# Self-attention scores by one mixed matrix, two-byte self parts, and an earlier load of two biases

## The reference

```python
# x: [1, 2048, 256]; every part is x = x + part(layernorm(x))
input_norm = norm(h, axis=-1); scaled = h / (input_norm + 1e-9)
q = scaled @ Wq.T + bq;  v = scaled @ Wv.T + bv
scores = q @ (q @ A).T / sqrt(256)                 # one head, width 256
ctx = softmax(scores) @ v;  out = ctx * input_norm
# cross-attention: 4 heads of width 64, keys and values from ctx_1024
# feed-forward: idx = argmax(softmax(x @ Wg + bg));  y = gelu(x @ W1[idx] + b1[idx]) @ W2[idx] + b2[idx]
```

## Time and profile before

| | |
|---|---|
| median of 3 runs | 823.52 us (822.39 to 825.96) |
| profiled execution | 824.94 us, of which the span of instructions 823.0 us |
| mean granted TensorE clock | 0.977 of full speed |
| PE busy | 760.4 us (92%) |
| PEld busy | 686.0 us (83%) |
| DVE busy | 629.1 us (76%) |
| ACT busy | 457.3 us (56%) |
| POOL busy | 165.5 us (20%) |

### The profile page before, as it was taken

The page is one execution under the profiler, slowest core; times in us unless marked ns, Lnnn a source line. Parts: engine busy times, 40 slices in busy tenths (PEclk is TensorE's granted clock), DMA queues, the critical chain, the costliest instruction groups (busy, mean ns, idle before and its releaser), DMA issues. The chain is left out here.

```text
span 823.0 us, 19881 instructions
## 1 busy us (share of the span) xinstructions
PE 760.4 (92%) x6226; PEld 686.0 (83%) x6227; DVE 629.1 (76%) x1608; ACT 457.3 (56%) x930; POOL 165.5 (20%) x254
## 2 busy tenths in 40 slices
PE   3878889999999999999999999999997768999996
PEld 2768779899898898988988889899895657999996
DVE  4983746797898888888889888888886754777773
ACT  2554536666766667666666666666664612444342
POOL 3100121212303123031230312303212011222221
PEclk9999989999999999999999999999999959999999
DMA  6233233213233131231312314213189290111110
GB/s 218 72 106 108 64 131 121 102 33 109 61 112 106 38 111 62 97 106 38 123 61 85 106 38 131 76 62 106 39 288 368 88 335 27 37 41 39 39 33 15
DMA packets 51146, 80.94 MB, mean 98 GB/s; under 512 B 4894, under 2 KB 29216, under 8 KB 50976
## 3 DMA queue, kind: packets, MB, share of 16 engines
q1 hardware_dynamic: 49232, 75.63, 27.2%
q0 software_dynamic: 1872, 4.76, 1.6%
HBM read 45.60 MB, written 35.18 MB: 98 GB/s over the span
## 5 line engine op out<-in xcount | busy, mean ns | idle before, releaser
L1135 ACT ACTIVATE ps_cross<-flip 128x512 f16<-128x512 f32 (+1 forms) x256 | 124.8, 515 | 110.4 <-PE flip L847 89.3
L1360 DVE TENSOR_TENSOR ps_cross<-flip,ps_cross 128x512 f16<-128x512 f32 (+1 forms) x256 | 145.0, 584 | 29.4 <-ACT ps_cross L1135 28.5
L1321 ACT ACTIVATE exp_cross<-exp_cross,xneg 128x1024 f32<-128x1024 f32 (+1 forms) x128 | 122.7, 960 | 28.0 <-DVE xneg L1520 28.0
L847 PE MATMUL flip<-ident,exp_cross 128*128 128x128 f32 (+1 forms) x832 | 130.9, 280 | 6.7 <-DVE ps_cross L1360 3.6
L836 PE MATMUL scores<-keys_cross,qt 128*128 128x402 f32 x512 | 126.8, 369 | 4.9 <-DVE xneg L1520 3.1
L847 PEld LDWEIGHTS flip<-ident,exp_cross 128*128 128x128 f32 (+1 forms) x832 | 95.2, 142 | 14.2 <-DVE ps_cross L1360 5.1
L724 PE MATMUL scores<-keys_self,u_tile 128*128 128x512 f32 x384 | 102.2, 403 | 4.3 <-issue 2.4
L823 PE MATMUL flip<-vals_self,ps_self 128*128 128x256 f32 x768 | 104.1, 290 | 0.0
L858 PE MATMUL cross_out<-vals_cross,ps_cross 128*128 128x128 f16 (+1 forms) x832 | 100.6, 222 | 0.2 <-DVE ps_cross L1360 0.2
L823 PEld LDWEIGHTS flip<-vals_self,ps_self 128*128 128x128 f32 x768 | 97.2, 195 | 0.0
L860 PE MATMUL cross_out<-vals_cross,ps_cross 128*128 128x64 f16 (+1 forms) x832 | 94.0, 194 | 0.0
(11 more groups left out here) (199 smaller groups left out, 1210.4 us busy)
## 6 DMA issues: line engine op xcount, KB each, us to landing
rows_dram<-pads SPq DMA_DIRECT2D x17, 520.0 KB, 4.0
w_piece<-W SPq DMA_DIRECT2D x32, 256.0 KB, 2.9
w_dram<-w_high SPq DMA_DIRECT2D x32, 256.0 KB, 2.3
w_dram<-w_piece SPq DMA_DIRECT2D x32, 256.0 KB, 2.7
w1s<-w_dram SPq DMA_DIRECT2D x8, 1024.0 KB, 12.4
w2s<-w_dram SPq DMA_DIRECT2D x8, 1024.0 KB, 12.5
...
```

Source lines behind the costliest of these rows:

```text
L847: tr = pe.transpose(flip[0:rows, bank(use), n * P:(n + 1) * P], exp_cross[:, h % 2, m * P:m * P + rows], ident[:, :])
L1135: return act.activation(out, in_, ACT.Copy, **kw)
L1321: act.activation(exp_cross[:, h % 2, cols], exp_cross[:, h % 2, cols], ACT.Exp, bias=xneg[:, h % 2, 1:2], scale=-1.0, accum_out=xden[:, ha ...
L1360: return dve.tensor_tensor(out, full, hi, ALU.subtract)
```

## The change

The score q A q' is written as x (Wq' A Wq) x' with a bias: in the prologue TensorE transposes Wq, multiplies A's matrix with it (`mixed[:, 0]`) and that with Wq again (`mixed[:, 1]`, with the factor 1/16), each with high and low parts, and two small products give u's bias `mixed_bias`. The parts of the transposed rows themselves are the keys: `xt_pro` goes, ScalarE and VectorE write them to `keys_self`, and the key matmuls and their parts go. u is mixed x x plus its bias. The values of group 0 come between the two products, and the statistics of group 1 ahead of the scaling of group 0.

`vals_self` and `ps_self` hold two-byte parts. The values are scaled by a number from a bound on them (row sums of squares of Wv, a sum over partitions by a matmul, a square root on GpSimd, the largest bv), the probabilities by 16384; the norms are multiplied by the inverse. `ps_self` has four buffers. b1 and b2 are loaded right after the prologue, behind the first piece's load, in a space of their own.

```diff
@@ -145,10 +146,11 @@
-    vals_self = sb("vals_self", [P, T, 2, D], F32R, keep)
+    vals_self = sb("vals_self", [P, T, 2, D], F16, keep)
+    exp_self = sb("exp_self", [P, N], F32, keep)
+    ps_self = sb("ps_self", [P, 4, 2, 512], F16, keep)
...
...
@@ -498,6 +510,8 @@
+        sp.dma_start(b1_row[:, :], bass.AP(io["b1"].tensor, 0, [[0, P], [1, E * DF]])).then_inc(b_loaded, 16)
+        sp.dma_start(b2_row[:, :], bass.AP(io["b2"].tensor, 0, [[0, P], [1, E * D]])).then_inc(b_loaded, 16)
...
@@ -547,8 +561,6 @@
-        sp.dma_start(b1_row[:, :], bass.AP(io["b1"].tensor, 0, [[0, P], [1, E * DF]])).then_inc(b_loaded, 16)
-        sp.dma_start(b2_row[:, :], bass.AP(io["b2"].tensor, 0, [[0, P], [1, E * D]])).then_inc(b_loaded, 16)
...
@@ -614,6 +626,9 @@
         for g in range(4):
+            if g == 2:
+                pool.wait_ge(bound_step, 3)
+                pool.tensor_tensor(v_bound[:, 2:3], v_bound[:, 1:2], plus_half[:, 0:1], ALU.pow).then_inc(bound_rooted, 1)
...
@@ -741,35 +758,68 @@
         def flip_x_pro(g):
-                pe.wait_ge(rows_scaled, 4 * (g + 1))
+                    pe.wait_ge(rows_scaled, 4 * (g + 1))
+                    if g == 0:
+                        pe.wait_ge(rows_scaled, n + 1)
+        pe.wait_ge(self_w_loaded, 48)
+        for c in range(C):
+            for o in range(C):
+                tr = pe.transpose(scores[:, 0, o * D + c * P:o * D + (c + 1) * P], w_raw[:, 0, c, o * P:(o + 1) * P], ident[:, :])
+        tr.then_inc(wq_flipped, 1)
-        for g in range(GROUPS):
-            if g == 0:
-                pe.wait_ge(self_w_lo, 1)
-            pe.wait_ge(pro_xt_lo, C * (g + 1))
-            for o in range(C):
-                if g:
-                    pe.wait_ge(pro_q_lo, C * (g - 1) + o + 1)
-                three(scores[:, o, :], lambda a, c: w_self[:, 0, a, c, o * P:(o + 1) * P],
-                      lambda b, c: xt_pro[:, g % 2, b, c, :]).then_inc(pro_q_ready, 1)
+        pe.wait_ge(self_w_lo, 2)
+        for o in range(C):
+            mm = three(scores[:, 1, o * D:(o + 1) * D], lambda a, c: w_self[:, 2, a, c, o * P:(o + 1) * P],
+                       lambda b, c: w_self[:, 0, b, c, :])
+        mm.then_inc(mixed_ready, 1)
+        def self_v(g):
+            for n in range(4):
+                if g == 0:
+                    pe.wait_ge(self_w_lo, 3)
+                pe.wait_ge(pro_xt_lo, C * (g + 1))
+                if g and n % 2 == 0:
+                    pe.wait_ge(pro_v_biased, 4 * (g - 1) + n + 2)
+                three(scores[:, 2 + n // 2, (n % 2) * D:(n % 2 + 1) * D],
+                      lambda a, c: keys_self[:, a, c, (4 * g + n) * P:(4 * g + n + 1) * P],
+                      lambda b, c: w_self[:, 1, b, c, :]).then_inc(pro_v_ready, 1)
+        self_v(0)
+        pe.wait_ge(mixed_lo, 1)
+        for o in range(C):
+            mm = three(scores[:, 0, o * D:(o + 1) * D], lambda a, c: mixed[:, 0, a, c, o * P:(o + 1) * P],
+                       lambda b, c: w_self[:, 0, b, c, :])
+        mm.then_inc(mixed_ready, 1)
+        pe.wait_ge(bound_step, 2)
+        pe.matmul(cross_out[:, 0:1], ones[:, :], bound16[:, :], start=True, stop=True).then_inc(bound_summed, 1)
...
+        for o in range(C):
+            for c in range(C):
+                mm = pe.matmul(cross_out[:, 8 + o:9 + o], w_raw[:, 2, c, o * P:(o + 1) * P], bq_col[:, c:c + 1],
...
+        mm.then_inc(bias_mixed, 1)
+        flip_x_pro(1)
+        pe.wait_ge(mixed_bias_set, 1)
+        pe.wait_ge(bound_step, 3)
+        for o in range(C):
...
+            for c in range(C):
+                for part in range(2):
+                    mm = pe.matmul(cross_out[:, 16 + o:17 + o], w_self[:, 0, part, c, o * P:(o + 1) * P].bitcast(F32),
+                                   mixed_bias[:, 0, c:c + 1], start=(n == 0), stop=(n == 3))
...
+        mm.then_inc(bias_mixed, 1)
+        self_u(0)
+        for g in range(1, GROUPS):
+            self_v(g)
-            if g == 0:
-                pe.wait_ge(self_w_lo, 2)
-            for n in range(4):
-                if g and n % 2 == 0:
-                    pe.wait_ge(pro_v_biased, 4 * (g - 1) + n + 2)
-                three(scores[:, 2 + n // 2, (n % 2) * D:(n % 2 + 1) * D] , lambda a, c: xt_pro[:, g % 2, a, c, n * P:(n + 1) * P],
-                      lambda b, c: w_self[:, 1, b, c, :]).then_inc(pro_v_ready, 1)
...
@@ -820,7 +870,7 @@
-                    mm = pe.matmul(self_out[:, 0:D], ps_self[:, g % 3, a, n * P:(n + 1) * P], vals_self[:, m, b, :],
+                    mm = pe.matmul(self_out[:, 0:D], ps_self[:, g, a, n * P:(n + 1) * P], vals_self[:, m, b, :],
...
@@ -1135,8 +1185,10 @@
-        for n in range(3):
-            copy(w_self[:, n, 0, :, :], w_raw[:, n, :, :]).then_inc(self_w_hi, 1)
+        copy(w_self[:, 2, 0, :, :], w_raw[:, 2, :, :]).then_inc(self_w_hi, 1)
+        act.wait_ge(wq_flipped, 1)
+        copy(w_self[:, 0, 0, :, :], scores[:, 0, :].rearrange("p (c n) -> p c n", c=C)).then_inc(self_w_hi, 1)
+        copy(w_self[:, 1, 0, :, :], w_raw[:, 1, :, :]).then_inc(self_w_hi, 1)
...
@@ -1144,29 +1196,28 @@
-                act.activation(u_out[:, :, o, :], out[:, :].rearrange("p (t s) -> p t s", t=4), ACT.Copy,
-                               scale=1.0 / 16.0).then_inc(u_hi_ready, 1)
+                act.wait_ge(mixed_bias_set, 2)
+                act.activation(u_out[:, :, o, :], out[:, :].rearrange("p (t s) -> p t s", t=4), ACT.Identity,
+                               bias=mixed_bias[:, 1, o:o + 1]).then_inc(u_hi_ready, 1)
         def xt_hi_pro(g):
...
-                copy(xt_pro[:, g % 2, 0, c, :], flip[:, c, :]).then_inc(pro_xt_hi, 1)
+                copy(keys_self[:, 0, c, g * 512:(g + 1) * 512], flip[:, c, :]).then_inc(pro_xt_hi, 1)
-        act.wait_ge(biases_loaded, 64)
+        act.wait_ge(mixed_ready, 1)
+        copy(mixed[:, 0, 0, :, :], scores[:, 1, :].rearrange("p (c n) -> p c n", c=C)).then_inc(mixed_hi, 1)
+        act.wait_ge(mixed_ready, 2)
+        copy(mixed[:, 1, 0, :, :], scores[:, 0, :].rearrange("p (c n) -> p c n", c=C), scale=1.0 / 16.0).then_inc(mixed_hi, 1)
         for g in range(GROUPS):
-            for o in range(C):
-                act.wait_ge(pro_q_ready, C * g + o + 1)
-                act.activation(keys_self[:, 0, o, g * 512:(g + 1) * 512], scores[:, o, :], ACT.Identity,
-                               bias=bq_col[:, o:o + 1]).then_inc(pro_q_hi, 1)
-                copy(vals_self[:, 4 * g + n, 0, :], v_tmp[:, n % 2, :]).then_inc(pro_v_hi, 1)
+                act.wait_ge(self_scale_step, 2)
+                act.activation(vals_self[:, 4 * g + n, 0, :], v_tmp[:, n % 2, :], ACT.Copy,
+                               scale=self_scale[:, 0:1]).then_inc(pro_v_hi, 1)
...
@@ -1219,11 +1270,9 @@
         def self_hi(j, k, g):
-            if g == 3:
-                act.wait_ge(self_p_used, 4 * j + 1)
-            elif k >= 1:
-                act.wait_ge(self_p_used, 4 * j if g == 0 else 4 * j + g - 3)
-            copy(ps_self[:, g % 3, 0, :], flip[:, bank(("s", g)), :]).then_inc(self_p_hi, 1)
+            if k >= 1:
+                act.wait_ge(self_p_used, 4 * j + g - 3)
+            copy(ps_self[:, g, 0, :], flip[:, bank(("s", g)), :], scale=P_TOP).then_inc(self_p_hi, 1)
...
@@ -1390,39 +1439,64 @@
         def xt_lo_pro(g):
-                low(xt_pro[:, g % 2, 1, c, :], flip[:, c, :], xt_pro[:, g % 2, 0, c, :].bitcast(F32)).then_inc(pro_xt_lo, 1)
+                low(keys_self[:, 1, c, g * 512:(g + 1) * 512], flip[:, c, :],
+                    keys_self[:, 0, c, g * 512:(g + 1) * 512].bitcast(F32)).then_inc(pro_xt_lo, 1)
-                                         scalar=1.0 / 16.0, in1=u_out[:, :, o, :].bitcast(F32), op0=ALU.mult,
+                                         scalar=mixed_bias[:, 1, o:o + 1], in1=u_out[:, :, o, :].bitcast(F32), op0=ALU.add,
-        for n in range(3):
-            if n == 1:
-                scale_rows(0)
-            dve.wait_ge(self_w_hi, n + 1)
-            low(w_self[:, n, 1, :, :], w_raw[:, n, :, :], w_self[:, n, 0, :, :].bitcast(F32)).then_inc(self_w_lo, 1)
-            if n == 1:
-                xt_lo_pro(0)
-                statistics_pro(1)
+        statistics_pro(1)
+        scale_rows(0)
+        dve.wait_ge(self_w_hi, 1)
+        low(w_self[:, 2, 1, :, :], w_raw[:, 2, :, :], w_self[:, 2, 0, :, :].bitcast(F32)).then_inc(self_w_lo, 1)
+        dve.wait_ge(self_w_hi, 2)
+        low(w_self[:, 0, 1, :, :], scores[:, 0, :].rearrange("p (c n) -> p c n", c=C),
+            w_self[:, 0, 0, :, :].bitcast(F32)).then_inc(self_w_lo, 1)
+        xt_lo_pro(0)
+        dve.wait_ge(self_w_hi, 3)
+        low(w_self[:, 1, 1, :, :], w_raw[:, 1, :, :], w_self[:, 1, 0, :, :].bitcast(F32)).then_inc(self_w_lo, 1)
+        dve.wait_ge(mixed_hi, 1)
+        low(mixed[:, 0, 1, :, :], scores[:, 1, :].rearrange("p (c n) -> p c n", c=C),
+            mixed[:, 0, 0, :, :].bitcast(F32)).then_inc(mixed_lo, 1)
```

(98 more changed lines are left out.)

9 lines of the change are left out of this document (4 added, 5 removed).

## The result

The changed kernel took **826.85 us** (median of 20 runs) against 822.68 us (median of 20 runs of the kernel before): **1.0036 times** the time before, with a 95% interval of 1.0025 to 1.0047, or +3.0 us. The ratio leaves disturbed executions out, the medians don't. The forecast was 823.2 us and no change: the time lies inside the range, but the slowing was not forecast. The profiled execution took 824.5 us (span 822.3, granted clock 0.968), 0.4 us *less* than the one of before.

The account below looks back on a forecast made before the run. Steady tiles were taken as bound by TensorE's self_values ahead of x1, the prologue by VectorE's queue, then a DMA round. Front +4.9, self parts -5.2, biases 0: -0.3, forecast 823.2 us, no change; range 817.8 to 830.

Parts of the forecast that it names:

- biases in tile 0: Loading b1 and b2 early on SP's queue in tile 0: 6.7 us at 389 GB/s, u_tile(1) in time, cost 0.
- The burst holds tile 1: Rival: the early b1 and b2 loads make tile 1's scores wait, +6 us, 829.2 us; chance 0.04.
- Self parts: Steady tiles: two-byte self_values matmuls at 113 ns for 120 save 0.31 us a tile ahead of x1, -5.2 us together.
- two bytes no faster: Rival, 48 self_values matmuls a tile: still 118 ns or more apart, so -5.2 is lost, 828.4 us; chance 0.14.
- Front: Prologue up to tile 0's start: mixing chain and reordered statistics, less key work, make it +4.9 us later (+2.5 to +7.6).
- the walk: Prologue followed along VectorE's queue: group 0 ends at 40.2 (+5.2), group 1 +4.45, u's high part of group 3 +4.65.
- the clock's 1.25 us: Rival on the prologue: TensorE idles longer and gets 1.2 GHz, forecast as +2.9 us, 826.1 us; chance 0.12.
- The sum's base: Whole kernel: -0.3 on the profiled 824.94 us gives 824.6; that execution lies 1.4 over the median 823.52, so 823.2.

## Why the prediction was wrong, point by point

**The step that failed** is the one on the biases in tile 0: "Cost 0." It measured 0.0037 in the changed kernel (1.0036 for 0.9999) and 0.0059 in the kernel with 2-byte parts: 3 to 5 us, all of the change's loss. I followed SP's own queue to u_tile(1), and that was nearly right: that load took 10.5 us to land and was there at 117.0 (forecast 112), ahead of the scores at 120.6. What I never listed was who else had DMAs in flight. GpSimd's four stores are another queue, and the chain from them (GpSimd's low part, the piece's stores, the next piece, ScalarE's copy, q's parts) was already tight: in the trace of before, ScalarE's copy of piece 1 ended 25.7 us after the first scores and q's high part began at 25.6. There the wait for x1 of tile 0 held the piece's load, and the stores were 1.6 us ahead of it. "The burst holds tile 1" stood as a rival at 0.04, with the wrong path and 6 us where it was 3 to 5. Its chance was too small because I asked only whether the bytes fit, and by full bandwidth at that: 389 GB/s, where the 2 MB took 11.1 us to land.

**Self parts**: forecast -5.2, measured -6.1 (-4.2 to -8.0). The mechanism was right. The spacing was 109 ns, not 113: by the two blocks 0.45 us a tile came off where I had 0.31, of which 0.35 arrived at x1. With 109 ns for two bytes and 120 for four, "two bytes no faster" was wrong. The Trainium skill, in "TensorE: Matmul & The Clock Gate" (Back-to-back issue gap), gives N/2.4 + 2.5 ns, which it calls the gap of an isolated matmul: 109 for 256 columns. I set it aside for the rows; the traces agree with it for two bytes and not for four.

**Front**: forecast +4.9, measured +5.9 (3.8 to 8.2) alone; group 0 ended at 39.1 to 41.3 over the nine traces with the new front, forecast 40.2. By the profiled execution the walk was 0.7 to 0.9 us too long at each mark and the clock's 1.25 us, which I had put into a rival, filled the gap: that the first scores came within 0.4 us of the forecast was luck.

**The sum's base.** I took the profiled execution's excess over the median, 1.4 us, as a constant. The pair of profiles agreed with the forecast to 0.15 us, by luck, while the medians differed by 3 to 4: before's profile had 10.2 us at 1.2 GHz in tiles 0 and 1, as the changed kernel's has. All 14 traces, by the time that these two tiles took and by the time at 1.2 GHz in them:

| at 1.2 GHz in tile 0 | late loads, or the stores moved | early loads, the stores ahead |
|---|---|---|
| 3.4 us | 47.3 to 48.7 us (6 traces), no more in tile 1 | 53.1 and 54.0, another 6.8 in tile 1 |
| 6.8 us | 49.6 to 51.0 us (4 traces), another 3.4 in tile 1 | 51.9 and 52.2, another 3.4 in tile 1 |

So the longer stretch in tile 0 comes with early and with late loads, and what brings it stays open. In the first row the burst costs 4 to 7 us: TensorE waits 3.5 and 5.3 us for q's parts of tile 1, and the 6.8 us at the low clock are in that tile. In the second it costs 1 to 3: x1 of tile 0 ends 2 us later there (20.8 us after the first scores in the trace of before, 18.8 with the 2-byte parts alone) and holds the second piece's load anyway. The two profiles that I compared are both of the second row, the one in which the cost hardly shows.

**Not settled:** why GpSimd's low part starts 4.1 to 5.8 us after the last thing that it waits for by its semaphores with late loads and 6.5 to 9.1 with early ones (5 to 6 and 1 to 2 us behind the stores' last packet). With the stores behind it, 2.2 to 3.1 us are left. So the runs show that moving the stores moves it, and not how they hold it.
